# Reordering spreads, row-sums, first-layer halves and copies in a two-layer interaction network

## The reference

```
x0 = xk = emb                                   # (512, 26, 32)
for w, b in ((conv1_w, conv1_b), (conv2_w, conv2_b)):
    hp = einsum('bhd,bmd->bhmd', xk, x0)        # every xk row times every x0 row
    xn = sigmoid(einsum('oi,bid->bod', w, hp.reshape(-1, h * 26, 32)) + b)
    xk = xn[:, :64];  res.append(xn[:, 64:])    # half goes on, half is a result
cin_feat = concat(res).sum(-1)
```

## Time and profile before

| | |
|---|---|
| median of 3 runs | 473.79 us (473.73 to 473.85) |
| the profiled execution | 473.68 us, span 471.6 us |
| PE busy | 91% of the span |
| DVE busy | 68% |
| ACT busy | 35% |
| mean DMA rate | 136 GB/s |
| products of pair 0 begin | 34.3 us |
| tanh network begins | 398.6 us |

### The profile page before, as it was taken

How to read it: one execution, slowest core, us unless ns; L and a number is a source line. 1 busy time by engine, 2 the same in 40 slices (tenths; PEclk the granted TensorE clock), 3 DMA queues, 4 the chain that set the end, 5 groups by cost and what they waited for, 6 DMA issues and landing times.

```text
span 471.6 us, 4901 instructions
## 1 busy us (share of the span) xinstructions
PE 429.2 (91%) x1716; PEld 181.0 (38%) x1716; DVE 319.9 (68%) x356; ACT 162.8 (35%) x264; POOL 149.4 (32%) x146
## 2 busy tenths in 40 slices
PE   3586969969899999999999999999999989999998
PEld 3532312313333333333333333333333323888685
DVE  3109456578697797989797797979797797332111
ACT  3151151341533454352544454352533330111111
POOL 6515633060505051432406051334000074860000
PEclk9878887979999999999999999999999989999999
DMA  5475643727677676777776596786665560420000
GB/s 178 107 155 136 142 107 81 188 57 190 136 178 172 157 196 165 171 186 182 174 189 168 151 213 155 169 191 166 164 177 129 141 178 0 113 68 1 0 0 0
DMA packets 38302, 64.00 MB, mean 136 GB/s; under 512 B 19601, under 2 KB 22033, under 8 KB 38278
## 3 DMA queue, kind: packets, MB, share of 16 engines
q1 hardware_dynamic: 34694, 61.93, 52.7%
q0 software_dynamic: 3584, 1.76, 2.8%
HBM read 61.96 MB, written 1.71 MB: 135 GB/s over the span
## 4 chain that ended last, share of the span: by engine, by line
PE 80%; DVE 10%; issue 8%; ACT 1%; DMA 0%; DVEq 0%
PE conv L430 37%; PE conv L408 19%; PE ring L420 7%; PE conv L486 7%; PE ring L486 7%; DVE prod L689 5%; DVE copied L689 3%; PE ring L394 2%; ACT sq L528 0%; DMA idx_sb<-in_idx 0%; ACT xk L539 0%; DVE x L623 0%; PE conv L505 0%; PE conv L501 0%; PE conv L437 0%
## 5 line engine op out<-in xcount | busy, mean ns | idle before, releaser
L346 POOL DMA_INDIRECT emb<-in_table,rows x112 | 115.2, 1029 | 207.0 <-DMA laid<-emb 175.5
L689 DVE TENSOR_TENSOR prod<-ring,xk 128x1024 f32<-128x1024 f32 x112 | 133.0, 1217 | 64.9 <-PE ring L420 32.6
L430 PE MATMUL conv<-prod,w_sb 128*64 128x512 f32 x448 | 116.9, 637 | 0.2
L689 DVE TENSOR_TENSOR copied<-copied,xk 128x1024 f32<-128x1024 f32 x96 | 116.1, 1250 | 0.3
L430 PE MATMUL conv<-copied,w_sb 128*64 128x512 f32 x384 | 93.6, 607 | 2.9 <-DVE copied L689 2.9
L408 PE MATMUL conv<-sq,w_sb 117*128 117x512 f32 x192 | 93.0, 622 | 0.5 <-ACT res L541 0.5
L539 ACT ACTIVATE xk<-conv,const_sb 64x512 f32<-64x512 f32 x64 | 43.8, 684 | 125.2 <-PE conv L408 115.6
L528 ACT ACTIVATE sq<-ring 117x512 f32<-117x512 f32 x96 | 52.0, 597 | 61.0 <-PE ring L394 52.8
L420 PE MATMUL ring<-x,sel_sb 58*128 58x512 f32 x224 | 48.8, 479 | 13.3 <-DVE prod L689 11.5
L408 PEld LDWEIGHTS conv<-sq,w_sb 117*128 117x128 f32 x192 | 34.8, 194 | 57.9 <-issue 56.5
L430 PEld LDWEIGHTS conv<-copied,w_sb 128*64 128x64 f32 x384 | 28.0, 141 | 62.6 <-issue 51.8
(11 more groups left out here) (75 smaller groups left out, 293.4 us busy)
## 6 DMA issues: line engine op xcount, KB each, us to landing
copied<-laid SPq DMA_DIRECT2D x192, 256.0 KB
wpiece<-in_mlp SPq DMA_DIRECT2D x22, 256.0 KB
emb<-in_table,rows POOLq DMA_INDIRECT x112
raw<-laid SPq DMA_DIRECT2D x32, 52.0 KB
laid<-emb SPq DMA_DIRECT2D x16, 96.0 KB, 4.5
sel_f<-in_sel SPq DMA_DIRECT2D x1, 832.0 KB, 5.7
const_sb<-in_const SPq DMA_DIRECT2D x1, 626.0 KB, 4.1
w_sb<-in_w SPq DMA_DIRECT2D x1, 416.0 KB
```

What stands on the lines that cost most here:

```text
L346: pool.indirect_dma_start(out=emb[0:n, i, j, :], out_offset=None, in_=table, in_offset=bass.IndirectOffsetOnAxis(ap=rows[0:n, i, j:j + 1], ...
L430: mm = nc.tensor.matmul(conv[i % 2][c * HALF:(c + 1) * HALF, :], w2_sb[:, t, :], prod_of(r)[:, c, :], start=(t == 0), stop=(t == T2 - 1))
L689: nc.vector.tensor_tensor(prod_of(r)[:, :, :].rearrange("p c n -> p (c n)"), left[:, :, :].rearrange("p c n -> p (c n)"), xk[i % 2][:, :, ...
```

## The change

It alters the order of work, a count of unused matmuls and the grain of some waits.

```
+SPREADS_IN = (((0, 4), (0, 5)), ((0, 8), (0, 9)), ((0, 12), (1, 0)), ((1, 1),))
 SUMS_IN = ({1: ((1, 0), (1, 1)), 2: ((1, 2),)},
-           {0: ((1, 0), (1, 1)), 1: ((1, 2),), 3: ((2, 0),)},
-           {0: ((1, 1), (1, 2)), 3: ((2, 0), (2, 1))},
+           {0: ((1, 0), (1, 1)), 1: ((1, 2),), 2: ((2, 0),), 3: ((2, 1),)},
            {0: ((1, 2),), 2: ((2, 0),), 3: ((2, 1),)})
-L1_IN = ({2: 0, 3: 1}, {1: 0, 2: 1}, {1: 0, 2: 1}, {0: 0, 1: 1})
-X_LOW_AT, TURN_AT, FOLD1_AT, PIECE_AT = (12, 11, 9, 5), (9, 9, 9, 9), (5, 5, 7, 7), 11
-WARM = 60
+L1_IN = ({2: 0, 3: 1}, {1: 0, 2: 1}, {0: 0, 1: 1})
+X_LOW_AT, TURN_AT, FOLD1_AT, PIECE_AT = (12, 7, 5), 9, (5, 5, 7), 11
+WARM = 100
...
+        def squares_up_to(i, u, c):
+            return UT * c + u + 1 if i == 0 else 2 * (UT * i + u) + c + 1
...  (SP)
-            for n in range(RC):
+            for n in range(2):
                 copy(n)
             lay_out(1)
             fetch(1)
+            for n in range(2, RC):
+                copy(n)
...
-                    if i == 0 and k == 1:
+                    if i == 0 and k == 0:
                         lay_out(2)
                         fetch(2)
...  (PE, in sums_of)
-                if u == 0:
-                    pe.wait_ge(x_lo_done, 2 * (i + 1))
                 slot_free("sums", i, u)
                 for c in range(2):
+                    if u == 0:
+                        pe.wait_ge(x_lo_done, 2 * i + c + 1)
...  (PE, the start)
+            pe.wait_ge(w1_step, 4)
+            layer1(0, 0)
             pe.wait_ge(sel_done, 2)
             spread_tile(0)
             spread_tile(1)
-            pe.wait_ge(w1_step, 4)
-            layer1(0, 0)
             layer1(0, 1)
...  (PE, in each group)
+                    for j, u in sums_in(i, g):
+                        sums_of(j, u)
                     for r in spreads_in(i, g):
                         spread_tile(r)
-                    for j, u in sums_in(i, g):
-                        sums_of(j, u)
...  (ACT, pair 0)
-            for u in range(UT):
-                squares(0, u)
+            for c in range(2):
+                for u in range(UT):
+                    act.wait_ge(sums_done, u + 1)
+                    nc.scalar.activation(sq[0][0:UK, u, c, :], sums_bank(0, u)[0:UK, c, :], ACT.Square).then_inc(sq_done, 1)
```

More of the change, by code:

```diff
@@ L201, in sums_in @@
         def sums_in(i, g):
-            return [(i + ahead, u) for ahead, u in SUMS_IN[min(i, 3)].get(g, ()) if i + ahead < NPAIR]
+            return [(i + ahead, u) for ahead, u in SUMS_IN[min(i, 2)].get(g, ()) if i + ahead < NPAIR]
         def spreads_in(i, g):
-            if g + 1 < len(GROUPS):
-                return [T2 * i + t for t in GROUPS[g + 1] if t in SPREAD]
-            return [T2 * (i + 1) + t for t in GROUPS[0] if t in SPREAD and i + 1 < NPAIR]
+            return [T2 * (i + ahead) + t for ahead, t in SPREADS_IN[g] if i + ahead < NPAIR]
+        def squares_up_to(i, u, c):
+            return UT * c + u + 1 if i == 0 else 2 * (UT * i + u) + c + 1
         def spreads_up_to(r):
@@ L240, in build @@
             enter(("sums", 0, u))
-        for r in spreads_in(-1, len(GROUPS) - 1):
-            enter(("spread", r))
+        for t in range(2):
+            enter(("spread", t))
         for i in range(NPAIR):
             for g in range(len(GROUPS)):
+                for j, u in sums_in(i, g):
+                    enter(("sums", j, u))
                 for r in spreads_in(i, g):
                     enter(("spread", r))
-                for j, u in sums_in(i, g):
-                    enter(("sums", j, u))
         def l1_bank(i, c):
@@ L384, in slot_free @@
                 else:
-                    pe.wait_ge(sq_done, 2 * (UT * last[1] + last[2]) + 2)
+                    pe.wait_ge(sq_done, squares_up_to(last[1], last[2], 1))
             def sums_of(i, u):
-                if u == 0:
-                    pe.wait_ge(x_lo_done, 2 * (i + 1))
                 slot_free("sums", i, u)
@@ L406, in layer1 @@
                 for u in range(UT):
-                    pe.wait_ge(sq_done, 2 * (UT * i + u) + c + 1)
+                    pe.wait_ge(sq_done, squares_up_to(i, u, c))
                     mm = nc.tensor.matmul(l1_bank(i, c)[:, :], w1_sb[:, u, :], sq[i % 2][0:UK, u, c, :],
@@ L455, in _ @@
                 for g, tiles_now in enumerate(GROUPS):
+                    for j, u in sums_in(i, g):
+                        sums_of(j, u)
                     for r in spreads_in(i, g):
                         spread_tile(r)
-                    for j, u in sums_in(i, g):
-                        sums_of(j, u)
                     for t in tiles_now:
                         main(T2 * i + t)
-                    if g in L1_IN[min(i, 3)] and i + 1 < NPAIR:
-                        layer1(i + 1, L1_IN[min(i, 3)][g])
+                    if g in L1_IN[min(i, 2)] and i + 1 < NPAIR:
+                        layer1(i + 1, L1_IN[min(i, 2)][g])
             pe.wait_ge(lin_step, 1)
@@ L578, in _ @@
                 if i + 1 < NPAIR:
-                    for u in range((0, 1)[i - 1] if i < 3 else 2, UT):
+                    for u in range(0 if i == 1 else 2, UT):
                         squares(i + 1, u)
-                if i == 1:
-                    sigmoid(2, 0)
                 if i + 2 < NPAIR:
@@ L587, in _ @@
                 if i + 1 < NPAIR:
-                    for c in range(1 if i == 1 else 0, 2):
-                        sigmoid(i + 1, c)
+                    sigmoid(i + 1, 0)
+                    sigmoid(i + 1, 1)
                 if i + 2 < NPAIR:
-                    for u in range(1 if i == 1 else 2):
-                        squares(i + 2, u)
+                    squares(i + 2, 0)
+                    squares(i + 2, 1)
             act.wait_ge(l1_done, 2 * NPAIR)
@@ L692, in _ @@
                                             ALU.mult).then_inc(prod_done, 1)
-                    k = min(i, 3)
+                    k = min(i, 2)
                     if i == 0 and t == 3:
@@ L699, in _ @@
                         fold1_of(i)
-                    if t == (0 if i == NPAIR - 1 else TURN_AT[k]):
+                    if t == (0 if i == NPAIR - 1 else TURN_AT):
                         turn(i)
-                    if t == TURN_AT[k] and i:
+                    if t == TURN_AT and i:
                         fold2_of(i - 1)
```

## The result

The changed kernel takes 446.34 us (median of 4 runs, 444.92 to 447.80) for 473.78: ratio 0.9421, interval 0.9382 to 0.9459. Its profiled execution took 447.80 us, span 446.0, so 1.8 us lie around the span. The forecast was 448.0 with 444 to 455.5. Ratios leave out runs that lie more than 1.5% above the fastest of their kernel.

The account below looks back on a forecast made before the run. PE was taken as the bound, with some 0.6 us without work per pair, at the border of two pairs. Six terms sum to -26.55 us, with +0.85 for the lower clock, bringing 473.68 to 448.0; range 444 to 455.5.

Parts of the forecast that it names:

- term 5: Eleven steady steps: product 0 follows product 12 at once, PE's wait at the border goes; 0.75 us each, -8.25 us.
- rival (c): Border of two pairs: the wait stays in another form, product 1 ending too late for spread 5; 456.3 us, chance 0.08.
- Rival (d): Group 3: next pair's spread waits for product 9 ahead of four mains; slower, 480 us at 5 us DVE delay; chance 0.03.
- term 2: Pair 0: second layout issued earlier behind fewer copies, sums before spreads; 27.0 us in place of 31.7, -4.7 us.
- Rival (a): Second layout is not earlier, since it waited for the gathers and not the copies; 450.7 us, chance 0.12.
- term 3: Pair 1: mains start sooner, less low clock, but a new 3.3 us PE wait for squares; 30.65 for 34.65, -4.0 us.
- term 4: Pair 2: takes the steady order at full clock, 20.6 us from mains to mains for 24.7; -4.1 us.
- term 1: The start: 40 more warm-up matmuls keep the clock full, squares by chunks; first product at 30.55 for 34.34, -3.8 us.
- term 6: Last pair, bound by DVE: product 1 starts 0.9 after mains 8-11, one product may get clear of POOL; -1.7 us.
- rival (b): Clock: new waits at 56-60 and 80.5-83.7 keep PE at 1.2 GHz for longer stretches; 451.4 us, chance 0.14.
- the allowance of 0.85: Pair 0: +0.85 us against the savings for the lower clock, as mains 4-7 follow a mostly idle PE.

## Why the prediction was right

**The bound and the border (term 5).** The reading held: one wait at the border, released by product 1, made late by the spread behind four mains. The step went from 21.30 to 20.42, 0.88 where I took 0.75 and bounded it at 0.85. The idle time was priced at 0.6; the rest is PE's busy time, 20.41 for 20.68, because spreads 4 and 5 now run together: 0.27, where I took 0.15 and bounded it at 0.25. The experiment with spread 0 moved back is the proof; rival (c), that the wait stays, is out, though the margin was thin (product 1 ends at 110.95, spread 5 starts at 111.19: 0.24, forecast 0.15). Rival (d), slower by a wait for product 9, did not appear: PE has no wait at all in 111.5 to 336.

**Pair 0 (term 2).** 27.06 us for a forecast of 27.0; layout at 27.70 for 27.4. The size was right, but not what it was put down to: the layout stands first in the term, and the order alone gave the same 27.06 with the layout at 31.89. The earlier layout pays only as far as the start is earlier: with the copies back, and a first product at 32.24, it was worth the 1.14 us that DVE waited, where 2.7 were forecast for a first product at 30.55. Rival (a) is out. (It read its own row wrongly: before, the layout went out 7.6 us after the last gather's start, 32.71 - 25.10, and not 6.7; nothing in the sum rests on that.)

**Pairs 1 and 2 (terms 3, 4).** 30.7 and 21.1 for 30.65 and 20.6. The wait of 3.3 us for ACT's squares was forecast in place and length; that it costs its whole length is not shown, since moving the squares shortened the profiles by about 1 us. The clock fell where I charged it, but for 6.8 us and not 3.4 at the first place, with 6.25 us of work. So up to the wait pair 1 took 1.1 us more than forecast (mains 3.6 after the first product for 3.1, then 20.4 for 19.8), and behind the wait 1.0 less (3.5 for 4.45), where part of the second low stretch fell into pair 2 instead: that term 3 came out within 0.1 us is luck. The experiments also correct the account behind terms 2 to 4: the order alone brings pairs 0 to 2 down by 11.5 us, and tables and layout add little.

**The start (term 1): mis-sized.** -3.8 was forecast, -1.6 measured. The step that failed is "x is ready at 20.8 and 21.5". It took one landing of raw (2.1 us) for the rule, and had no bound for it; it was 4.5 in this execution and 2.1 to 4.5 over all. From the sums on, the step holds in this execution: from the time at which both low parts are ready to the first product 9.0 us (23.75 to 32.72) for 8.75 by the working, and 12.8 before (21.53, at the lower clock). But "I take the clock as full" had luck: of the eleven profiles with 100 warm-up matmuls the clock fell in the start (24.6 to 30.4) in five, and from x_high(0) to the first product these took 12.8 to 14.4 us for 11.1. (The warm-up matmuls stand 0.110 apart and not 0.114; the hundred ended at 21.77, as forecast.)

**The last pair (term 6).** -2.15 for -1.7. Product 1 came 0.5 us after mains 8-11, where I had 0.9 and it was 2.1 before: -1.6 for -1.2. From product 1 to main 12 it took 17.4 us for 18.2: -0.8, inside my 0 to -1.1. The mains before it came 0.2 later. By the Trainium skill (SBUF — State Buffer, "Who interferes with whom") a product ahead of POOL's first subtraction should be clear of it. The trace agrees, with 2.35 us for two products at 355.42 and 3.56 for two at 359.95, and the run without POOL's work agrees with the cause.

**The clock, rival (b).** It did not decide: the stretches at 1.2 GHz behind the two new waits were 6.8 and 3.4 us long, where rival (b) had them as long as the 10.2 us before. The time goes with the mean clock from run to run of one kernel. The Trainium skill (TensorE: Matmul & The Clock Gate, "What's actually happening") has activity release the throttle. The runs agree as far as they go: with unused matmuls in the wait at 61, all of 62.60 to 85.28 was at 2.4 GHz; one profile without them was too.

The sum was right by more than its parts: term 1 was 2.2 too good, term 4 0.5 too good, terms 5 and 6 together 1.9 too small, and the allowance of 0.85 covered what was left. The mechanism of the steady part is shown; that the profiled execution came within 0.2 us of the forecast is luck, as errors of 2 us cancelled and the same kernel runs from 444.92 to 449.81.

## What to carry to other kernels

Where in-order engines feed each other through a short ring of buffers, look for the one producer that stands behind a long block of work which doesn't need it: putting one spread of 0.4 us back behind four mains cost 12 of the 27 us. The new waits here came in the place and length that rows of the trace gave, but a single DMA's landing time did not: bound it by more than one row. A wait that goes is not worth its length when the next wait stands right behind it: taking 3.3 us of waiting out by ACT's order shortened the profiles by about 1 us. And repeat a gain of a few us before it is believed; one of 3.2 us, with intervals apart, was not there in the next six runs.

## What the runs showed that was not expected

- The landing of the same 52 KB transfers varied between 2.1 and 4.5 us from execution to execution, and was 3.3 us in the one with neither copies nor gathers beside them.
- The granted clock falls and rises at other times in each execution of one kernel. The same program ran at a mean clock of 0.981 to 1.0, and within 442.03 to 449.58 us. The kernel before, whose first runs lay inside 0.12 us, later spread over 3.6 us. So a few runs that agree are no measure of how well a kernel repeats.
- A stretch of 25.7 us took 3.0 us less at full clock, in one profile with matmuls of no use in front of it and in one of another variant without them. Seventeen such matmuls made the kernel no slower.
